# Weight integers kept in the order they are loaded, and the first rows of the second phase split: a quantised 3x3 residual block on one core

## The reference

```python
alpha_s = alpha * g + (alpha - alpha * g)            # g = 1 / sqrt(w.size * 3)
wq = round(clip(w / alpha_s, -4, 3)) * alpha_s       # integers of 3 bits, times a scale
out = conv3x3(x, wq1)                                # padding 1, stride 1
out = relu(batchnorm(out, gamma1, beta1))            # mean and variance over images and pixels
out = batchnorm(conv3x3(out, wq2), gamma2, beta2)
out = relu(out + x)
```

## Time and profile before

| | us |
|---|---|
| median of 3 runs | 1474.97 (1474.01 to 1475.03) |
| the profiled execution's own time | 1474.11 |
| its span in the profile | 1472.3 |
| PE busy | 1132.3 (77%) |
| DVE busy | 1145.5 (78%) |
| ACT busy | 854.4 (58%) |
| POOL busy | 462.5 (31%) |

### The profile page before, as it was taken

How to read it: one execution, slowest core, us unless ns; L and a number is a source line. 1 busy time by engine, 2 the same in 40 slices (tenths; PEclk the granted TensorE clock), 3 DMA queues, 4 the chain that set the end, 5 groups by cost and what they waited for, 6 DMA issues and landing times.

```text
span 1472.3 us, 19175 instructions
## 1 busy us (share of the span) xinstructions
PE 1132.3 (77%) x5802; PEld 1030.9 (70%) x5802; DVE 1145.5 (78%) x1562; ACT 854.4 (58%) x1263; POOL 462.5 (31%) x211
## 2 busy tenths in 40 slices
PE   5999999999999998899999999999999400000000
PEld 5999999999999997899999999999999400000000
DVE  8999999999999996988888888888888642223324
ACT  3655555655565556677777777777777532322224
POOL 3444444444444552433334333333333100000000
PEclk9999999999999999899999999999999755555555
DMA  4454454444452210022245455444230799999999
GB/s 163 157 191 188 189 193 174 174 174 174 174 191 106 96 44 0 0 89 87 93 186 196 184 194 191 179 174 174 87 131 16 277 429 430 431 429 429 430 429 409
DMA packets 28098, 296.83 MB, mean 202 GB/s; under 512 B 3888, under 2 KB 3888, under 8 KB 4912
## 3 DMA queue, kind: packets, MB, share of 16 engines
q1 hardware_dynamic: 22608, 245.25, 42.2%
q10 hardware_dynamic: 5472, 51.38, 8.2%
HBM read 174.59 MB, written 122.03 MB: 201 GB/s over the span
## 4 chain that ended last, share of the span: by engine, by line
issue 52%; POOL 26%; DMA 18%; DVE 1%; ACT 1%; POOLq 1%; ACTq 0%; DVEq 0%
POOL v_lo L417 26%; DMA slots<-conv_spill 11%; DMA out<-slots 4%; DMA xbuf<-in_x 3%; DVE slots L860 1%; ACT slots L611 1%; POOLq L422 1%; POOLq L416 0%; POOLq L77 0%; ACTq L615 0%; POOLq L417 0%; DVE affine L781 0%; DVE tiny L779 0%; DVE affine L782 0%; POOL ident L403 0%
## 5 line engine op out<-in xcount | busy, mean ns | idle before, releaser
L417 POOL TENSOR_TENSOR v_lo<-v_rows,v_hi 128x1008 fp32r<-128x1008 f32 x192 | 460.2, 2429 | 666.8 <-ACT v_hi L469 666.8
L913 PE MATMUL conv_psum<-d_hi,w2T 128*128 128x398 f32 (+2 forms) x864 | 286.6, 336 | 10.3 <-issue 10.3
L913 PE MATMUL conv_psum<-d_hi,w1T 128*128 128x398 f32 (+2 forms) x864 | 286.0, 335 | 2.6 <-ACT slots L488 1.5
L913 PE MATMUL conv_psum<-d_lo,w2T 128*128 128x398 f32 (+2 forms) x864 | 284.9, 334 | 0.0
L913 PE MATMUL conv_psum<-d_lo,w1T 128*128 128x398 f32 (+2 forms) x864 | 284.4, 333 | 0.0
L507 ACT ACTIVATE squares<-slots,minus_shift 128x1008 bf16 (+3 forms) x192 | 225.0, 1172 | 15.0 <-ACT squares L507 12.4
L893 PE MATMUL conv_psum<-v_lo,w1T 128*128 128x512 f32 x576 | 227.2, 394 | 0.0
L893 PE MATMUL conv_psum<-v_lo,w2T 128*128 128x512 f32 x576 | 227.2, 394 | 0.0
L893 PE MATMUL conv_psum<-v_hi,w2T 128*128 128x512 f32 x576 | 226.7, 394 | 0.0
L893 PE MATMUL conv_psum<-v_hi,w1T 128*128 128x512 f32 x576 | 226.6, 393 | 0.0
L860 DVE SCALAR_TENSOR_TENSOR slots<-slots,affine,xbuf 128x3136 f32<-128x3136 f32 (+1 forms) x30 | 97.4, 3265 | 160.9 <-DMA slots<-conv_spill 155.2
(11 more groups left out here) (78 smaller groups left out, 1457.5 us busy)
## 6 DMA issues: line engine op xcount, KB each, us to landing
conv_spill<-slots SPq DMA_DIRECT2D x44, 1568.0 KB, 6.1
slots<-conv_spill SPq DMA_DIRECT2D x44, 1568.0 KB, 10.8
slots<-in_x SPq DMA_DIRECT2D x31, 1568.0 KB, 8.9
out<-slots ACTq DMA_DIRECT2D x30, 1568.0 KB, 11.7
xbuf<-in_x SPq DMA_DIRECT2D x28, 1568.0 KB, 52.9
xbuf_w<-in_x SPq DMA_DIRECT2D x4, 1568.0 KB, 49.9
out<-slots ACTq DMA_DIRECT2D x4, 784.0 KB, 10.3
slots<-in_L_conv_w SPq DMA_DIRECT2D x2, 576.0 KB, 9.7
```

What stands on the lines that cost most here:

```text
L417: nc.gpsimd.tensor_tensor(pair_window(1, k), pair_rows(k), pair_window(0, k).bitcast(F32), ALU.subtract).then_inc(pool_lo_ready, 1)
L913: last = nc.tensor.matmul(bank_run(CHUNK_BANK[j], r1 - r0), w[:, kh * 3 + kw, :], run(d_plane[half], r0 - WINO + 1, r1 - WINO + 1, kw - 1) ...
```

## The change

Three parts.

1. `integer_taps` writes the integers in the order in which the weights come (channel, tap), without a stride. The transposes of the nine taps then read every ninth number (`int_plane`), and `sum_taps` reads three neighbouring taps of each channel and writes its result one matrix after the other, with 256 bytes between neighbouring taps.
2. The ReLU, `d_hi` and `d_lo` of the direct rows of the first image of phase 2 are made in two parts, rows 35 to 43 and rows 44 to 55 (`SPLIT` is 44), each with semaphores of its own. The first chunk on TensorE waits for the first part alone, the second chunk for both.
3. The two alphas are loaded by ScalarE's queue, ahead of gamma and beta, and no longer by SP's.

```diff
+    SPLIT = CHUNKS[0][1] + 1
...
         def integer_taps(k):
-            return nc.vector.tensor_scalar(w_int[k][:, 0:TAPS * C].rearrange("o (t c) -> o c t", t=TAPS),
-                                           w_raw[k].rearrange("o (c t) -> o c t", t=TAPS),
-                                           ROUND, None, ALU.subtract)
+            return nc.vector.tensor_scalar(w_int[k][:, 0:TAPS * C], w_raw[k], ROUND, None, ALU.subtract)
+
+        def int_plane(k, t):
+
+            if t < TAPS:
+                return w_int[k][:, 0:TAPS * C].rearrange("o (c t) -> o t c", t=TAPS)[:, t, :]
+            return w_int[k][:, t * C:(t + 1) * C]
...
-            g0, g1, g2 = (w_int[k][:, kh * 3 * C:(kh + 1) * 3 * C] for kh in range(3))
-            a, b, c, d = (w_int[k][:, (TAPS + 3 * j) * C:(TAPS + 3 * j + 3) * C] for j in range(4))
+            taps_of = w_int[k][:, 0:TAPS * C].rearrange("o (c t) -> o c t", t=TAPS)
+            g0, g1, g2 = (taps_of[:, :, kh * 3:kh * 3 + 3] for kh in range(3))
+            a, b, c, d = (w_int[k][:, (TAPS + 3 * j) * C:(TAPS + 3 * j + 3) * C].rearrange("o (kw c) -> o c kw", kw=3)
+                          for j in range(4))
...
-            for k, a in enumerate((alpha1, alpha2)):
-                sp.dma_start(alpha_in[:, k:k + 1], a.rearrange("(a n) -> a n", a=1).to_broadcast([C, 1])
-                             ).then_inc(alpha_landed, 16)
             sp.dma_start(w_raw[0], w1.rearrange("o c a b -> o (c a b)")).then_inc(w_landed[0], 16)
...
         def _(act):
+            for k, a in enumerate((alpha1, alpha2)):
+                act.dma_start(alpha_in[:, k:k + 1], a.rearrange("(a n) -> a n", a=1).to_broadcast([C, 1])
+                              ).then_inc(alpha_landed, 16)
...
             act.wait_ge(affine_ready, 1)
-            relu(0, 0)
+            relu_rows(WINO - 1, SPLIT).then_inc(first_relu_ready, 1)
+            act.wait_ge(first_relu_ready, 1)
+            act.wait_ge(chunk_done, IMAGES * NC)
+            hi_rows(WINO - 1, SPLIT).then_inc(first_hi_ready, 1)
+            relu_rows(SPLIT, H).then_inc(relu_ready, 1)
             act.wait_ge(relu_ready, 1)
-            hi_direct(IMAGES, SPILL)
+            hi_rows(SPLIT, H).then_inc(hi_ready, 1)
...
-            lo_direct(IMAGES, SPILL)
+            dve.wait_ge(first_hi_ready, 1)
+            lo_rows(WINO - 1, SPLIT).then_inc(first_lo_ready, 1)
+            dve.wait_ge(hi_ready, IMAGES * HI + 1)
+            lo_rows(SPLIT, H).then_inc(lo_ready, 1)
...
-                                               w_int[k][:, t * C:(t + 1) * C], ident[:, :])
+                                               int_plane(k, t), ident[:, :])
...
             def chunk(g, j, w):
+                if isinstance(g, int) and g == IMAGES and j == 0:
+                    pe.wait_ge(first_lo_ready, 1)
+                elif j == 0 or (isinstance(g, int) and g == IMAGES and j == 1):
+                    pe.wait_ge(lo_ready, g * LO + 1)
```

More of the change, by code:

```diff
@@ L157, in residual_block @@
         relu_ready = sem("relu_ready")
+        first_relu_ready = sem("first_relu_ready")
+        first_hi_ready = sem("first_hi_ready")
+        first_lo_ready = sem("first_lo_ready")
         m_done = sem("m_done")
@@ L580, in _, with relu_rows, hi_rows @@
             act.wait_ge(affine_ready, 1)
-            relu(0, 0)
+            def relu_rows(r0, r1):
+                y = slot(SPILL, r0, r1)
+                return nc.scalar.activation(y, y, ACT.Relu, bias=affine[:, 0, 1:2], scale=affine[:, 0, 0:1])
+            def hi_rows(r0, r1):
+                return nc.scalar.copy(window(d_plane[0], r0 - (WINO - 1), r1 - (WINO - 1)), rows_of(slot(SPILL, r0, r1)))
+            relu_rows(WINO - 1, SPLIT).then_inc(first_relu_ready, 1)
[3 more added lines that the diff above has]
+            relu_rows(SPLIT, H).then_inc(relu_ready, 1)
             act.wait_ge(relu_ready, 1)
-            hi_direct(IMAGES, SPILL)
+            hi_rows(SPLIT, H).then_inc(hi_ready, 1)
             relu(0, 1)
@@ L834, in phase2, with lo_rows @@
                 step(m + IMAGES, m + SPILL, b, 1, first, relu_over)
-            lo_direct(IMAGES, SPILL)
+            def lo_rows(r0, r1):
+                part = [window(plane, r0 - (WINO - 1), r1 - (WINO - 1)) for plane in d_plane]
+                return nc.vector.tensor_tensor(part[1], rows_of(slot(SPILL, r0, r1)), part[0].bitcast(F32),
+                                               ALU.subtract)
+            dve.wait_ge(first_hi_ready, 1)
+            lo_rows(WINO - 1, SPLIT).then_inc(first_lo_ready, 1)
+            dve.wait_ge(hi_ready, IMAGES * HI + 1)
+            lo_rows(SPLIT, H).then_inc(lo_ready, 1)
             dve.wait_ge(relu_ready, NR)
@@ L902, in chunk @@
             def chunk(g, j, w):
+                if isinstance(g, int) and g == IMAGES and j == 0:
+                    pe.wait_ge(first_lo_ready, 1)
+                elif j == 0 or (isinstance(g, int) and g == IMAGES and j == 1):
+                    pe.wait_ge(lo_ready, g * LO + 1)
                 if j == 0:
-                    pe.wait_ge(lo_ready, g * LO + 1)
                     if not (isinstance(g, int) and g == 0):
```

## The result

The changed kernel takes 1482.07 us (median of 5 runs, 1481.57 to 1483.24), the kernel before 1474.38 beside it (5 runs, 1473.88 to 1475.03). The ratio is 1.0053, with a 95% interval of 1.0038 to 1.0068: slower by 7.7 us, where 0.35 had been forecast, and 3.4 us past the upper end of the range. The profiled execution took 1481.57, with a span of 1479.7 against 1472.3.

What follows compares the result with a forecast made beforehand. It took VectorE's chain to bound TensorE's start, and ScalarE's chain with GpSimd behind it to bound the gap between the phases. Terms: +0.75 at the start, -0.4 between phases, +0.35 in all, 1475.3 us; range 1472.4 to 1478.7.

Steps and rivals of the forecast that it cites:

- sums of taps with a stride: VectorE at the start: six sums written 256 bytes apart at 1.02 us each, 2.8 us more in all.
- The chain: What sets TensorE's start: VectorE's alpha, clip, round, integers, `d_lo`, six sums, `q_rows`; start forecast +0.75 us.
- (c): Sums at their upper bound, 1.4 to 1.88 us each: +3 to +5.5 us, 1478 to 1480.5; chance 0.12.
- alpha: Start, loads by ScalarE's queue: w1 issued first, the clip's wait for it goes, a gain of 0.3 us.
- (e): At the start alpha comes late, sharing the DMA engines with w1: +1.4 to +2.4 us; chance 0.05.
- The integers without a stride: VectorE at the start: integers written in a row cost about what the rounding does, gain 1.56 us.
- `d_lo`: VectorE at the start: runs 1.58 us there against 1.39 elsewhere; 0.2 us counted as gained.
- The strided reads: TensorE's transposes reading every ninth number, for w1 and w2: zero cost, covered on both sides.
- six sums of w2 in phase 1: VectorE in phase 1's steps: one sum dearer by 0.46 us fits; by 1.3 would only just be caught up.
- Between the phases: Direct rows split: TensorE starts 1.87 us earlier, ReLU of 1960 0.47 later, GpSimd is awaited; gain 0.4 left.
- (b): TensorE's clock falls in the longer pause at the start: 2.9 us lost, 1478.2 in all; chance 0.2.
- (d): Strides nearly free in the sums: start gains 2.05 us, the whole -2.45, 1472.5; chance 0.18.

Runs made afterwards that it cites:

- the single measurement: Seventeen VectorE instructions on zeros put at the start of the kernel before, measured once: 1491.79 us; a sum written with 256 bytes between neighbours took 1.873.

## Why the prediction was wrong

**The step that failed is "sums of taps with a stride".** The chain was right, and so was the place, and no step behind it failed; the term was mis-sized, 2.8 taken, 7.64 measured in the changed kernel (1.88 us for a sum against 1.02). That is close to the upper bound I had worked out (8, or 1.88 for a sum), with a reason beside it that fits: that the integers ran two numbers at a time. I then chose by the likeness of the writes ("exactly the way the sums now write") and overlooked that the price depends on the instruction too. The rows to doubt it by were there: the rounding, f32 without a stride, takes less than 0.7 ns a number, a sum takes (0.557 - 0.16) / 384 = 1.03. An instruction that handles one number in the time in which the other handles two could not be given the other's price for a number. Per pair, the integers' row says 4.5 ns, and six sums at 4.5 are the measured time. Rival (c) should have been the forecast.

That the sum's strided bf16 write costs 4.5 ns is measured. That this is so because the integers are written in pairs is argued from the factor of two and not shown: no run gives the two instructions the same types, and with f32 a strided number costs 1.72 ns in the sum and 1.05 in the subtraction, a factor of 1.6.

**Second, alpha.** Forecast -0.3, measured +1.72 here and +1.74 alone. The landing time was read from a queue beside which no byte of w1 moved in the first 5 us; in the changed kernel w1 is issued at the same moment as the alphas, and its bytes flow before 2 us. Rival (e) named just this, at +1.4 to +2.4, and had 0.05. With SP's loads held back the alphas are there at 4.50, with them beside at 8.49.

**Together**: +1.72 - 1.68 - 0.21 + 7.64 = +7.47, +0.2 in `q_rows`, -0.2 between the phases, which makes +7.5; the spans differ by 7.4, the medians by 7.7. The rivals were priced one at a time, and the range had no room for two at once: (c) ends at 1480.5, and with alpha 2.0 later than forecast that makes 1482.5, against 1482.07. (The lower end of (c) has a slip: -2.05 + 5 - 0.4 is +2.5, not +3.)

**What held.** The integers without a stride take 0.76, the gain is 1.68 (1.56 forecast). `d_lo` gives 0.2. The strided reads cost the transposes next to nothing: w1's first nine take 1.15 in place of 1.12, w2's 21 take 1.43 in place of 1.35, with 0.219 for one in both. Of the six sums of w2 in phase 1 five take 1.92 to 1.96, 1.3 more than the 0.62 before, and one takes 3.90, and phase 1 still has no pause; its end is late by 7.70, as its start is by 7.68. Between the phases the start is 1.81 sooner (1.87), the ReLU 0.52 later (0.47), GpSimd is waited for (1.10 in one wait, 1.4 forecast), and 0.40 is left at the third piece (0.4). At the end of phase 2 only 0.2 of it shows, and alone 0.13, too little to measure.

**Of the other rivals.** (b) named the clock: it did fall, but cost nothing, since the chunk behind the pause ends 0.8 before ScalarE begins to empty the bank that the third chunk needs. The 2.9 priced for it overlooked that wait. And it is no cause but a consequence: the pause grew because the sums were late. (d), strides nearly free, falls with the 1.873 of the single measurement.

**Open**: whether the integers really are written in pairs; why one sum of w2 takes 3.90; and what in SP's queue delays ScalarE's tiny loads, its packets' bytes or the work of having them under way.

## What to carry to other kernels

Price a stride by the instruction that will have it, not by the one that had it: first ask how many numbers each handles at a time (its time without a stride, per number), then how far neighbouring writes lie apart. Moving a stride from a writer to readers can win (here 1.7 us with all writes in a row, where the readers are transposes and sums by threes), but it depends on the reader: the integers' own instruction would have paid 2.20 in place of 2.74. Moving it to another writer, six sums with twice the numbers in all, lost 6. A tiny load that a chain starts from did best alone ahead of the large one (5.38), worst as a pair beside it (8.46). And a consumer that starts 1.8 us sooner is worth only what the next late engine leaves of it, here 0.1 to 0.4; look for the next wait one image further on too.

## What the runs showed of the hardware

- The cost of a strided bf16 write grows with its step, up to 16 bytes: 0.589 us for 384 numbers at 4 bytes, 1.010 at 8, 1.856 at 16, 1.873 at 256, against 0.557 in a row. The Trainium skill, Advanced Engine Details and Errata, SBUF Cachelines, names lines of 16 bytes and asks for two hits in a line for full speed. The measured price hardly grows beyond a step of 16, which agrees; but with two hits a line (8 bytes) it is already 0.45 us more, and there the measurement decides.
- In the sums reads are another matter: with 256 bytes between neighbours, three columns going round, 0.559; in steps of 18 bytes, 0.85. In the integers' instruction a read in steps of 36 bytes takes 2.196, against 0.760 in a row. And a sum of f32 written 512 bytes apart takes 0.820, less than half of bf16. The section makes no difference between reads and writes. It does say that the tolerance of strides depends on the type of number, and the f32 row agrees, though it gives no price.
- Two loads of 128 packets of 4 bytes were there 4.0 us later with large loads beside them on another queue (8.49 against 4.50). That fits packets of the two queues taking turns, 33 and 29 of them in one microsecond, but is not shown to be all of it, since 145 against 820 packets of ScalarE's queue moved in the first 5 us even where SP's queue had moved only small ones. The two loads' own bytes, 512 each, did not tell when they would land.
